# Moving a transpose and a piece of an expert product behind the second half of the first attention scores

## The reference

```python
h = tok(x, W0, b0, pos0, W1, b1, pos1, W2, b2, pos2, scale_emb)   # (16, 221, 128)
h = h + attn(layernorm(h), w_qkv, w_agg, b_agg)
h = h + ffn(layernorm(h), expert_weights, expert_indices, w1, w2)

def attn(z, w_qkv, w_agg, b_agg):
    q, k, v = einsum('bnd,ed->bne', z, w_qkv) ...                 # 8 heads of 16
    attn = softmax(q @ k.T / sqrt(16))
    return einsum('bnd,ed->bne', attn @ v, w_agg) + b_agg

def ffn(x, ...):                                                  # per expert e
    y = gelu(x[rows of e] @ w1[e]) @ w2[e]
    out[token] += weight * y
```

## Time and profile before

| | |
|---|---|
| time, median of 3 runs | 252.54 us (252.16 to 252.75) |
| the profiled execution: its time, its span | 252.67 us, 250.0 us |
| TensorE busy | 239.3 us, 96% of the span |
| vector, scalar, GpSimd engine busy | 185.1, 138.9, 133.7 us |
| TensorE's share of the chain that ended last | 86% |
| granted TensorE clock | 1.000 of full speed |

### The profile page before, as it was taken

The page is one execution under the profiler, slowest core; times in us unless marked ns, Lnnn a source line. Parts: engine busy times, 40 slices in busy tenths (PEclk is TensorE's granted clock), DMA queues, the critical chain, the costliest instruction groups (busy, mean ns, idle before and its releaser), DMA issues.

```text
span 250.0 us, 6983 instructions
## 1 busy us (share of the span) xinstructions
PE 239.3 (96%) x2703; PEld 198.8 (80%) x2703; DVE 185.1 (74%) x417; ACT 138.9 (56%) x223; POOL 133.7 (53%) x181
## 2 busy tenths in 40 slices
PE   7999899999999999999998999999999999999992
PEld 6899879777686788797777888888888888877671
DVE  3898646959796879788765786878787877866743
ACT  4771230744344343544464958787877778787450
POOL 7000066140747465767574375867777877673422
PEclk9999999999999999999999999999999999999999
DMA  6999603314638483942415318272636363535222
GB/s 208 409 393 399 273 21 92 86 25 91 206 84 241 96 244 88 240 118 59 119 33 131 90 22 163 33 162 34 134 60 151 47 141 42 122 41 116 37 21 47
DMA packets 30192, 32.00 MB, mean 128 GB/s; under 512 B 3831, under 2 KB 26695, under 8 KB 30129
## 3 DMA queue, kind: packets, MB, share of 16 engines
q1 hardware_dynamic: 25214, 28.17, 39.4%
q0 software_dynamic: 4080, 2.59, 8.2%
q10 hardware_dynamic: 866, 0.81, 1.0%
HBM read 16.24 MB, written 5.95 MB: 89 GB/s over the span
## 4 chain that ended last, share of the span: by engine, by line
PE 86%; DMA 4%; DVE 4%; issue 2%; ACT 1%; POOL 1%; DVEq 0%
PE s_ps L1288 16%; PE e_ps L1212 14%; PE s_ps L1212 11%; PE m_ps L1405 9%; PE e_ps L1485 8%; PE m_ps L1471 5%; PE m_ps L1273 5%; PE e_ps L1471 2%; PE m_ps L1279 2%; PE m_ps L1434 2%; DMA w_raw<-wt 2%; DMA z_slots<-z,slot_u 1%; PE m_ps L1262 1%; PE m_ps L1280 1%; PE m_ps L1435 1%
## 5 line engine op out<-in xcount | busy, mean ns | idle before, releaser
L994 DVE TENSOR_REDUCE nmax<-s_ps 104x4 fp32r<-104x884 f32 (+1 forms) x60 | 61.9, 1073 | 10.1 <-PE s_ps L1288 9.9
L684 ACT ACTIVATE probs<-s_ps 104x888 f32<-104x888 f32 (+1 forms) x60 | 51.2, 905 | 26.8 <-PE s_ps L1288 26.7
L571 POOL DMA_INDIRECT out<-y_sb,idx_u x23 | 36.4, 1582 | 33.5 <-DMA out<-y_sb,idx_u 26.3
L1288 PE MATMUL s_ps<-pair_a 32*104 32x222 f32 (+1 forms) x504 | 37.8, 307 | 0.5 <-ACT probs L684 0.5
L1288 PEld LDWEIGHTS s_ps<-pair_a 32*104 32x104 f32 (+1 forms) x504 | 24.5, 169 | 13.7 <-issue 8.8
L501 POOL TENSOR_TENSOR var_eps<-mv,eps_t 128x2 f32<-128x2 f32 x16 | 6.0, 378 | 49.0 <-DVE mv L959 48.9
L534 POOL DMA_INDIRECT z_slots<-z,slot_u x20 | 22.1, 1107 | 15.2 <-PE s_ps L1288 11.3
L1405 PE MATMUL m_ps<-probs,v_aug 104*32 104x221 f32 (+1 forms) x480 | 25.8, 353 | 0.0
L1485 PE MATMUL e_ps<-w_now,hidT 128*128 128x128 f32 x184 | 23.2, 276 | 0.0
L1485 PEld LDWEIGHTS e_ps<-w_now,hidT 128*128 128x128 f32 x184 | 21.7, 192 | 0.2
L745 ACT ACT_TABLE_LOAD x16 | 20.5, 1283 | 0.3
(11 more groups left out here) (165 smaller groups left out, 532.8 us busy)
## 6 DMA issues: line engine op xcount, KB each, us to landing
pair_a<-qk SPq DMA_DIRECT2D x64, 111.0 KB
w_sb<-w SPq DMA_DIRECT2D x8, 512.0 KB, 4.3
pair_b<-qk SPq DMA_DIRECT2D x30, 111.0 KB
w_raw<-wt SPq DMA_DIRECT2D x6, 512.0 KB, 10.5
x_raw<-x SPq DMA_DIRECT2D x6, 512.0 KB, 9.4
z_slots<-z SPq DMA_DIRECT2D x1, 1518.0 KB, 13.5
zs<-z_slots SPq DMA_DIRECT2D x7, 198.0 KB, 3.3
x_raw<-x SPq DMA_DIRECT2D x4, 256.0 KB, 4.7
```

The costliest lines, as they stand in the source:

```text
L571: g.indirect_dma_start(rows, bass.IndirectOffsetOnAxis(ap=idx_u[:, at:at + 1], axis=0), y_sb[:, n % 2, i, :], None, compute_op=ALU.add).th ...
L684: s.activation(probs[0:n, blk, 2 * f:2 * f + 2].rearrange("p t u n -> p t (u n)"), s_ps[0:n, 2 * f:2 * f + 2, 0:2 * NE], ACT.Exp, scale=DH ...
L994: v.tensor_reduce(nmax[0:n, blk, 2 * f:2 * f + 2, MAX_ROW[0]:MAX_ROW[1] + 1:2], src, AX_X, ALU.max, negate=True).then_inc(max_ready, 1)
L1288: mm = pe.matmul(dst[0:n, i, u * NE:(u + 1) * NE], a[rs, u, N0 * blk:N0 * blk + n], b[rs, u, :], start=start, stop=stop)
```

## The change

On TensorE, the second half of the first scores (after the embedding steps `p0`, which only cycle 0 has in that place) comes right behind p times v. z's turn, h's turn (for `n < 0`) and the quarter of an expert product (for `n > 0`) follow it, ahead of `project_qk`. On the scalar engine the copy of z's turn stands behind the copy of p times v in all cycles. Nothing else differs; because the file loses lines, line numbers on TensorE are two lower in the changed kernel.

```diff
@@ scalar engine
                 weigh_y(n - 1)
-                if n <= 0 <= c + 1:
-                    zT_copy(c + 1)
                 if c - 1 >= 0:
                     o_raw_copy(c - 1)
-                if n > 0 and c + 1 < BATCH:
+                if 0 <= c + 1 < BATCH:
                     zT_copy(c + 1)
@@ TensorE
                 if here:
                     s1(c, 0)
-                if ahead1 and n <= 0:
-                    z_turn(c + 1)
                 if behind:
                     pv(c - 1)
-                if ahead1 and n > 0:
-                    z_turn(c + 1)
-                if n > 0:
-                    hidden(n, 0, FC - 1, FC)
                 tok_some(p0)
                 if here:
                     s1(c, 1)
+                if ahead1:
+                    z_turn(c + 1)
+                if ahead2 and n < 0:
+                    h_turn(c + 2)
+                if n > 0:
+                    hidden(n, 0, FC - 1, FC)
                 if n == 0:
                     zs_turn(0)
                 if ahead1:
@@
                 hidden(n, 1)
                 hidden(n, 2)
-                if ahead2 and n < 0:
-                    h_turn(c + 2)
                 tok_some(p1)
```

## The result

The changed kernel takes 259.63 us, median of its four runs, beside 252.64 for the kernel before in the same comparison. One run of each was slow (440.10 and 258.90 us; without them the medians are 259.40 and 252.54), and so were the traced executions of the two experiments that move h's turn in the kernel before, of which only cycles at a granted clock of 1.00 are used. The ratio is 1.029, with a 95% interval of 1.024 to 1.034: slower by 7.3 us (6.1 to 8.5). The direction and the mechanism hold; the size was 3 us too large.

The account below looks back on a forecast made before the run. TensorE's queue was taken to bound each cycle; 6 x 0.72 + 6 x 0.82 + 0 - 0.1 + 0.6 + 0.4 = 10.1 us on 252.54 gave 262.6 us, range 259.8 to 264.4.

Parts of the forecast that it names:

- The maxima hold the second half's end: First scores: the second half's end stays tied to the first half's maxima; starting earlier gains 0 and 0.03 us.
- Rival 1: First scores: the maxima come in time, the second half isn't held, so 256.8 us; chance 0.07.
- rival 3: Later in the cycle: slack swallows the stall, so no change, 252.5 us; chance 0.03.
- The gap of 0.85: From z's turn to the projection of q and k: turn, copy and restart take 0.85 us without cover.
- the 0.25 to 0.45 that I had named as a sign: Idle TensorE in us at the projection's wait for z's copy, expected in each of some 14 cycles.
- The cycles with experts: Cycles 8 to 13: the quarter saves nothing in the gap, so each cycle costs 0.85 - 0.03 = 0.82 us.
- Rival 4: Scalar engine: the first Gelu delays the cast of q and k, 3.7 us more, so 266.3 us; chance 0.05.
- h's turn, saved at 0.13: Cycles 1 to 6: moving h's turn into the gap saves 0.13 us, so each cycle costs 0.72.
- Cycle 14: sized at 0.4: Cycle 14: the vector engine paces TensorE, which waits 0.31 and 0.32; cost between 0.2 and 0.5 us, taken as 0.4.
- My range: Whole kernel: 259.8 to 264.4 us, leaving out the rivals, 2 in 10.
- Rival 2: TensorE: one visit to the full array fewer in 13 cycles gains 2.7 us, so 249.8 us; chance 0.05.
- the 0.21 of the prediction: TensorE: cost in us of a visit from strips to the full array, z's turn at 0.34 against h's at 0.13.

Follow-up runs that it names:

- Short maxima: Maxima over half of the columns, 1.14 us long instead of 2.06: ratio 1.007 in the changed kernel, 1.009 in the kernel before.
- again: A second execution of each kernel, unchanged: 254.98 us for the kernel before, 260.51 us for the changed kernel.
- the second run of the first experiment: The changed kernel with the order of before for `n > 0`, so the change in cycles -1 to 7 alone: ratio 1.015 (1.007 to 1.023).

## Why the prediction was right in direction, and 3 us too large

*The maxima hold the second half's end: right.* Last heads 0.06 behind them in both kinds of cycle, gains of 0 and 0.03 as forecast (the second maxima of cycle 9 begin 3.52 us into the cycle for 3.55). Short maxima release it by 0.53, so the tie is shown by an experiment. Rival 1 falls by this, and rival 3 by the ledger.

*The gap of 0.85: right*, measured 0.85 and 0.84, taken from a single occurrence in cycle -1; with nothing in it, cycle 2 pays 0.85. The idle time listed is 0.20 or 0.21, below the 0.25 to 0.45 that I had named as a sign, since what was put into the gap counts as busy; bare, it is 0.43.

*The cycles with experts: right*, 0.81 each for 0.82. Rival 4 falls too: the Gelu runs at 164.75 for 0.60, and the cast starts 1.06 behind the projection (165.96), as before.

*h's turn, saved at 0.13: the step that failed.* I read its price from its own first start to the next instruction's start. But its first transpose starts 0.85 behind the projection (69.38 to 70.23), where an embedding step starts 0.69 behind it: part of the price lies ahead of h's own rows. The price is how far the work behind it moves when h's turn is gone: 0.23 to the embedding's second product. The cycle kept 0.21 of it. Six cycles at 0.08 more are 0.5. Most of the rest lies in cycles 3 and 4, which cost only +0.49 and +0.50, against a forecast for cycles 1 to 6 that was 0.84 too high in all. There TensorE was already held in the kernel before, at the placed maxima: they start 5.44 us into cycle 3, 0.06 behind the end of the second half's maxima, and the next step follows 0.27 behind their start, 0.17 in the changed kernel. The delay takes up that wait, 0.13 in each of the two cycles. It is not listed as idle, and I had looked for no such wait.

*Cycle 14: sized at 0.4, measured 0.96* (0.78 again). I had set TensorE's two waits there against the gap. What happened is elsewhere: the maxima of cycle 14 start 1.41 us after its scores instead of 0.70, since the normalisation of that input was late. The order of time of the changed kernel there:

```profile
227.53 1.57 POOL L571 DMA_INDIRECT out<-y_sb,idx_u  x1 [3.81 <-PE s_ps L1286]
228.55 0.79 POOL L501 TENSOR_TENSOR var_eps<-mv,eps_t 128x2 f32<-128x2 f32 x1
...
230.18 0.60 DVE L962 TENSOR_SCALAR z_sb<-h_sb,mv,rstd 128x128 f32<-128x128 f32 x2 [1.59 <-POOL rstd L503]
230.70 2.06 DVE L992 TENSOR_REDUCE nmax<-s_ps 104x4 fp32r<-104x884 f32 x2
```

POOL's `var_eps` stands behind a scatter of results. The row names the second scores as its releaser, but the half that this scatter waits for by the code was through at 224.0; the scatter ahead of it, for which it also waits, was issued at 220.97 and took 5.8 us to land (4.0 in the kernel before). In the run with h's turn behind the projection, whose order is the same from cycle 8 on, it landed after 4.8 us, the maxima started after 0.70, and cycle 14 costs only +0.27 (11.66). And with the order of before from cycle 8 on (the second run of the first experiment) the maxima were as late, 1.41, and cycle 14 took 11.87, +0.48 without any change in it. So the late maxima cost about 0.5 to 0.7, and the new order 0.27 (11.66 for 11.39) to 0.48 (12.35 for 11.87), about the 0.4 that I had sized. Why that transfer takes longer I haven't settled.

*What was left out: the variation of the rest.* Of the 10.1 forecast, the cycles 0 to 14 without 7 account for 9.88. Cycle 7, the start, the last store and the time outside the span gave 0.65 + 0.26 + 0.94 + 0.83 = 2.7 back in this pair of executions, and the first two at least vary so much with the same program. My range allowed for costs of the change only, not for this. That it is all chance is not shown: the timed runs, with 7.3 (6.1 to 8.5), don't reach 9.9 either. How much of the change's cost the rest of the program takes back stays open. My reading of the waits also passed over four of 0.7 to 1.0 us, at about 1, 6, 30 and 245 us of the span; they lie outside cycles 0 to 14 and change no term of the sum.

*Rival 2, one visit to the full array fewer.* A visit does cost something, less than I took, and it doesn't decide. p times v follows the first half 0.34 us earlier than before (0.62 into the cycle for 0.96), and with h's turn behind p times v two transposes between strips cost 0.35 (70.54 to 70.89). Among full-size products h's turn costs 0.23, not 0.13, so the visit itself costs 0.11 or 0.12, about half of the 0.21 of the prediction, and the rival would have gained 13 x 0.12 = 1.6 us, not 2.7. The Trainium skill, page "TensorEngine Tiling (Array Packing)", section "Key Properties", states that a change of the tiling mode drains TensorE; that small difference agrees with it. The 0.34 us saved only lengthened the wait for the maxima.

## What to carry to other kernels

Work that stands between a producer and a wait is free there; before moving it, find the wait that hides it, even where no idle time is listed, and price the new place by its own latency (transpose, copy and restart: 0.85 us here). Price a moved instruction by how far the work behind it moves, the second instruction behind it too, not by its own rows. And before filling a shadow further, look for the second and third limit: here the maxima and the bank of p times v allowed the projection within 0.02 us of each other, and the second half's maxima left 0.2 us of room ahead of their placing, or none (cycles 3 and 4).

## What the hardware showed that I hadn't expected

The scatter of results ahead of cycle 14 took 5.8 and 5.7 us to land in two executions of the changed kernel, 4.8 in one with the same order from cycle 8 on, and 3.8 to 4.8 in six with the order of before there. The loads ahead of cycle 7 moved the same program by 1.2 us. And a whole visit from strips to the full array, with two transposes in it, has cost 0.34 or 0.35 us in each of three places: z's turn before, h's turn behind p times v, and p times v's earlier start after. Two transposes among full-size products cost 0.23.
